# Attention weights of a graph network: one copy and one subtraction for a unit's transposed weights, where there were two of each

## The reference

```python
def _sparse_attention(x, src, dst, wq, bq, wk, bk, wv, bv, wo, bo):
    N, D = x.shape
    H, Dh = (NUM_HEADS, D // NUM_HEADS)          # 4 heads of 128
    q = (x @ wq + bq).reshape(N, H, Dh) * Dh ** (-0.5)
    k = (x @ wk + bk).reshape(N, H, Dh)
    v = (x @ wv + bv).reshape(N, H, Dh)
    scores = jnp.einsum('ehd,ehd->eh', q[src], k[dst])
    smax = jax.ops.segment_max(scores, src, num_segments=N)
    ex = jnp.exp(scores - smax[src])
    denom = jax.ops.segment_sum(ex, src, num_segments=N)
    attn = ex / denom[src]
    out = jax.ops.segment_sum(attn[:, :, None] * v[dst], src, num_segments=N)
    return out.reshape(N, D) @ wo + bo

for i in range(NUM_BLOCKS):                      # 4
    y = _cond_layer_norm(x, cond, s1_w[i], s1_b[i], b1_w[i], b1_b[i])
    x = x + _sparse_attention(y, src, dst, wq[i], ..., bo[i])
    y = _cond_layer_norm(x, cond, s2_w[i], s2_b[i], b2_w[i], b2_b[i])
    x = x + jax.nn.relu(y @ m_w1[i] + m_b1[i]) @ m_w2[i] + m_b2[i]
```

## Time and profile before

| | |
|---|---|
| median of 3 runs | 1796.01 us (1793.98 to 1800.16) |
| the profiled execution | 1803.08 us, of which the span from the first to the last instruction is 1801.3 us |
| mean granted TensorE clock | 0.988 of full speed |
| TensorE matmuls / weight loads busy | 1736.3 us (96%) / 1529.9 us (85%) |
| VectorE busy | 1244.6 us (69%) |
| ScalarE busy | 791.8 us (44%) |
| GpSimd busy | 588.7 us (33%) |
| subtraction of the weights, L1218 | 320 times, 243.9 us |
| copy of the weights, L982 | 320 times, 202.4 us |

### The profile page before, as it was taken

The page is one execution under the profiler, slowest core; times in us unless marked ns, Lnnn a source line. Parts: engine busy times, 40 slices in busy tenths (PEclk is TensorE's granted clock), DMA queues, the critical chain, the costliest instruction groups (busy, mean ns, idle before and its releaser), DMA issues.

```text
span 1801.3 us, 32290 instructions
## 1 busy us (share of the span) xinstructions
PE 1736.3 (96%) x11886; PEld 1529.9 (85%) x11886; DVE 1244.6 (69%) x2198; ACT 791.8 (44%) x1304; POOL 588.7 (33%) x892
## 2 busy tenths in 40 slices
PE   6999997899999999999999999999999999999998
PEld 5997786788999888879998888799987887999877
DVE  5998557736787668357776783577767835778676
ACT  4553432124666341246664412366644213666531
POOL 1003454402333534023334540123346401233383
PEclk9999998999999999999999999999999999999999
DMA  4002400221111212121212121211121122112221
GB/s 130 1 1 88 167 36 30 87 97 45 45 60 31 80 64 87 52 71 31 60 46 82 41 87 61 81 34 52 53 83 41 43 106 72 39 45 60 61 94 69
DMA packets 64714, 113.07 MB, mean 63 GB/s; under 512 B 15254, under 2 KB 25622, under 8 KB 64576
## 3 DMA queue, kind: packets, MB, share of 16 engines
q1 hardware_dynamic: 64576, 111.22, 19.1%
HBM read 89.19 MB, written 22.00 MB: 62 GB/s over the span
## 4 chain that ended last, share of the span: by engine, by line
PE 81%; DVE 10%; issue 4%; ACT 2%; DVEq 2%; POOL 1%; DMA 1%; SPq 0%; POOLq 0%; ACTq 0%
PE ps L1500 55%; PE ps L1561 14%; PE ps L1646 6%; PE ps L1587 2%; PE ps L1601 2%; DVE masked_s L1234 1%; DVE hot L1067 1%; DVE x L1271 1%; PE ps L1458 1%; DVE mask_log L1107 1%; DVE stat L1088 1%; DVE hot L1070 1%; DVE mask_out L1112 1%; ACT mask_log L857 1%; POOL rstd L637 1%
## 5 line engine op out<-in xcount | busy, mean ns | idle before, releaser
L1218 DVE TENSOR_TENSOR pT<-ps,pT 128x640 fp32r<-128x640 f32 (+1 forms) x320 | 243.9, 804 | 154.4 <-ACT pT L982 154.4
L1500 PE MATMUL ps<-yT,w 128*128 128x512 f32 (+1 forms) x1728 | 330.4, 352 | 1.3 <-DVE y L1355 1.3
L1500 PE MATMUL ps<-kh,q_parts 128*128 128x512 f32 (+3 forms) x1440 | 315.8, 363 | 10.2 <-DVE small L1234 7.0
L1500 PEld LDWEIGHTS ps<-yT,w 128*128 128x128 f32 x1728 | 280.5, 189 | 46.6 <-DVE y L1355 1.7
L982 ACT CAST pT<-ps 128x640 fp32r<-128x640 f32 (+1 forms) x320 | 202.4, 685 | 252.9 <-PE ps L1646 242.3
L1500 PEld LDWEIGHTS ps<-kh,q_parts 128*128 128x128 f32 (+1 forms) x1440 | 243.9, 185 | 58.2 <-issue 6.0
L1500 PE MATMUL ps<-w,kh 128*128 128x512 f32 (+1 forms) x960 | 240.5, 402 | 8.0 <-DVE x L1333 4.4
L1500 PEld LDWEIGHTS ps<-w,kh 128*128 128x128 f32 (+1 forms) x960 | 177.8, 190 | 48.4 <-DVE x L1333 5.3
L919 ACT ACTIVATE s<-masked_s,small 128x1280 f32 (+1 forms) x156 | 214.9, 1378 | 0.0
L1561 PE MATMUL ps<-pT,v 128*128 128x256 f32 (+1 forms) x1600 | 214.2, 280 | 0.0
L1561 PEld LDWEIGHTS ps<-pT,v 128*128 128x128 f32 x1600 | 199.5, 190 | 0.0
(11 more groups left out here) (188 smaller groups left out, 2596.2 us busy)
## 6 DMA issues: line engine op xcount, KB each, us to landing
mask<-mask_dram SPq DMA_DIRECT2D x24, 640.0 KB, 5.1
x_spill<-x SPq DMA_DIRECT2D x36, 256.0 KB
x<-x_spill SPq DMA_DIRECT2D x36, 256.0 KB, 4.6
rep<-rec_dram SPq DMA_DIRECT2D x64, 128.0 KB, 3.3
w_raw<-in_L_gnn_m_w_dram SPq DMA_DIRECT2D x8, 1024.0 KB, 6.0
mask_y<-mask_dram SPq DMA_DIRECT2D x12, 640.0 KB, 5.3
mask_dram<-mask_out SPq DMA_DIRECT2D x10, 640.0 KB, 2.9
x<-in_x_dram SPq DMA_DIRECT2D x2, 2304.0 KB
```

Source lines behind the costliest of these rows:

```text
L1218: nc.vector.tensor_tensor(pT[:, 1, places, k * P:k * P + R], turn_bank(half, R), pT[:, 0, places, k * P:k * P + R].bitcast(F32), ALU.subtr ...
L1500: mine = mm(to, left(a), right(b), start=first and n == 0, stop=final and n == 2)
```

## The change

The two halves are joined. ScalarE copies all 1280 columns of a unit in one instruction, and VectorE subtracts in one. Both use patterns that name the two runs of 640 columns in PSUM (`turn_banks`), and the two runs of five places in `pT` (`turned_weights`: a step of one half, or of two, by the parity of `gh`). Each semaphore now counts one for a unit instead of two, and TensorE's waits are rewritten: both parts of `weigh`, and both halves of the transposes, wait for the same count.

```diff
+        def turn_banks(R):
+            both = ps_flat[:, 3 * BANK:7 * BANK].rearrange("p (h b) -> p h b", h=2)[:, :, 0:NT // 2 * P]
+            return both.rearrange("p h (t r) -> p h t r", r=P)[:, :, :, 0:R]
+
+        def turned_weights(n, gh, k, R):
+            thirds = pT[:, n, :, :].rearrange("p (h t) r -> p h t r", t=NT // 2)
+            return thirds[:, 0:2 + gh % 2:1 + gh % 2, :, k * P:k * P + R]
...
                     act.wait_ge(turned, i * U + u + 1)
-                    for half in range(2):
-                        nc.scalar.copy(pT[:, 0, turned_places(gh, half), k * P:k * P + R], turn_bank(half, R)).then_inc(p_high, 1)
+                    nc.scalar.copy(turned_weights(0, gh, k, R), turn_banks(R)).then_inc(p_high, 1)
...
-                for half in range(2):
-                    places = turned_places(gh, half)
-                    dve.wait_ge(p_high, (i * U + u) * 2 + half + 1)
-                    nc.vector.tensor_tensor(pT[:, 1, places, k * P:k * P + R], turn_bank(half, R),
-                                            pT[:, 0, places, k * P:k * P + R].bitcast(F32), ALU.subtract).then_inc(p_ready, 1)
+                dve.wait_ge(p_high, i * U + u + 1)
+                nc.vector.tensor_tensor(turned_weights(1, gh, k, R), turn_banks(R), turned_weights(0, gh, k, R).bitcast(F32),
+                                        ALU.subtract).then_inc(p_ready, 1)
...
                 wd = rows(2 * g) + rows(2 * g + 1)
-                weights = (i * U + 2 * gh + 1) * 2 + part + 1
+                weights = i * U + 2 * gh + 2
                 pe.wait_ge(p_high, weights)
...
                         if u >= 1:
-                            pe.wait_ge(p_ready, (i * U + u - 1) * 2 + half + 1)
+                            pe.wait_ge(p_ready, i * U + u)
```

## The result

The changed kernel took 1808.97 us (median of 5 runs, 1807.74 to 1811.91), the kernel before 1794.40 us (5 runs, 1793.95 to 1800.16). The ratio is 1.0078, with a 95% interval of 1.0059 to 1.0097: slower by 0.6 to 1.0%, 14.6 us by the medians. (Against the 1796.01 us named ahead, the median of the first three of these runs, it is 13.0 us.) In a second comparison it was 1.0071 (1.0049 to 1.0094). The profiled execution of the changed kernel took 1807.74 us, its span 1806.0.

The account below looks back on a forecast made before the run. TensorE was taken as the bound, delayed by VectorE's later mask. Per block, 3.0 us for 16 pairs plus 0.9 for two dear pairs made 3.9, over four blocks 15.6: 1811.6 us on the median, range 1807 to 1816 (8-in-10: 1799 to 1822).

Parts of the forecast that it names:

- The bound, and who is late: In attention, TensorE bounds at 4.40 us a unit; its next scores wait for VectorE's mask, queued behind the subtraction.
- The lateness: The rest (copied value subtracted from the turned one) is ready 2.74 us after the copy's start, not 2.28: 0.46 later.
- The signal's time and the slack: Mask to TensorE's weight load: 0.12 us signal, leaving true slack of 0.37 after an even unit, 0.26 after an odd.
- Two short waits that do not add: Ordinary pair of units loses max(0.20, 0.09) = 0.20 us; the weighing's third-pass stall of 0.10 to 0.17 is absorbed.
- rival 2: Nothing absorbed: the weighing's 0.13 us stall adds to each pair's 0.20, giving 1820.8 us; chance 0.12.
- The dear pairs: Two pairs per block where VectorE also splits output-weight quarters ahead of the mask: no slack, the whole 0.46 us paid.
- The transposes' wait: TensorE's transposes waiting on the rest cost nothing: they load at 492.55, the rest is there at 491.99.
- The sum: Per block 16 x 0.19 = 3.0 plus 2 x 0.46 = 0.9, together 3.9 us; over four blocks 15.6 us.
- What I said the views would show: New trace: pair 9.0 us instead of 8.80, TensorE not busy throughout 82 us, mask and subtraction on the wait chain.
- rival 1: Slack covers ordinary pairs; only the dear pairs pay, 8 x 0.46 = 3.7 us, giving 1799.7 us; chance 0.15.
- rival 3: Joined two-piece operations save no fixed part: rest 0.77 us late, 9.7 us a block, 1834.8 us; chance 0.06.
- rival 4: Faster: the path from copy through exponential to transposes decides, each unit gains 0.06 us, 9.6 in all, 1786.4; chance 0.05.

Follow-up runs that it names:

- Both delays: Kernel before plus one unrelated VectorE maximum per unit ahead of the mask, over 128 or 384 columns: ratios 0.9991 and 1.0073.
- only the copy joined: Kernel before with ScalarE's copy joined into one instruction, VectorE still subtracting in two halves behind it: 1815.39 us, ratio 1.0098.
- The third trace: Unchanged kernel before, traced a third time to see whether half-clock stretches recur: 421.8 us ahead of the first attention stage.

## Why the prediction was right

The forecast was 15.6 us slower, 1811.6 us on the median; 1808.97 was measured, 14.6 us slower than the kernel before, and it lies in the forecast's own range of 1807 to 1816. By its steps:

**The bound, and who is late.** Right. The delay put into the kernel before shows it without the change: a mask 0.46 us later costs 16.2 of the 16.7 us in the stages, at unchanged copies, rests and waits.

**The two durations.** 1.23 and 1.485 us were taken, 1.230 and 1.492 measured.

**The lateness.** 0.46 us was forecast; 2.75 - 2.28 = 0.47 measured.

**The signal's time and the slack.** 0.12 us was taken for the signal, from a unit in mid-stage. The masks' signals against the weight loads give 0.10 behind every odd unit, so odd slack is 0.26 us. Both delays agree: 0.19 is free in ordinary pairs, and 0.46 costs 0.19 a pair on average.

**Two short waits that do not add.** 0.20 a pair was forecast, 0.20 measured (9.00 for 8.80). The stall at the third pass was there, 0.10 us, the low end of its 0.10 to 0.17, and it was inside the other wait: without it the pair is shorter by less than 0.01. So rival 2 falls. The wait was spread, in the changed kernel, almost evenly over both units (4.51 and 4.49), which I had not pictured; the sum is the same.

**The dear pairs.** 0.46 each was forecast, 0.49 measured.

**The transposes' wait.** It was put at nothing, from a unit in mid-stage. In the last unit of each block, where no scores come in between, that is wrong:

```profile
597.53 1.03 PE L1646 MATMUL ps<-ident,s 98*128 98x98 f32 x10 [0.99 <-ACT s L919]
```

```profile
596.46 1.01 PE L1651 MATMUL ps<-ident,s 98*128 98x98 f32 x10 [1.20 <-DVE pT L1223]
```

In the kernel before (first line) these transposes wait for the exponential, in the changed one for the rest of the unit before. The unit takes 3.94 us for 3.76, 0.7 us over the four blocks.

**The sum.** 3.9 us a stage was forecast, 4.2 measured. The two dear pairs have 0.98 of it for the forecast's 0.92, and everything else 3.2 for 3.0, the last unit's 0.18 included. The four stages have 16.7 us, and the time has 14.6; the missing 2 us lie outside attention, where executions differ by more than that. So the total came closer to the forecast than the stages alone make it: nothing was forecast outside attention, where the changed kernel met fewer half-clock stretches. For the forecast, that is luck.

**What I said the views would show** was wrong in two points: TensorE is still busy in all of the 82 us, and the mask is not on the chain of waits of ordinary units. The mechanism is there, and these views are too coarse for it.

The other rivals: the slack does not cover ordinary pairs (rival 1), the joined operations are not dearer (rival 3), and nothing ran through the exponential in mid-stage (rival 4). Rival 4's gain exists in the last unit of a block, where "only the copy joined" takes 3.71 us for 3.76.

## What to carry to other kernels

Two instructions that hand work from one engine to the next in halves overlap; joined, each engine works less and the result comes later. Before joining, follow the result to the engine that is the bound, through everything queued behind it on the way, and compare the added lateness with the slack there: here a lateness up to that slack was free, beyond it each pair of units paid the difference (0.47 - 0.26 forecasts 0.21, and 0.20 was measured), and two waits on one loop counted once. The cheap test is to delay the suspect by a foreign operation of known length, in two sizes, one below the slack and one above it.

## What the runs showed of the hardware that was not expected

The pattern of two pieces was a risk (rival 3) and cost nothing. A copy out of PSUM and a subtraction that read two runs of 640 columns, 1024 apart, and write ten pieces of 128, took 1.230 and 1.492 us: the copy as long as one that reads 1280 contiguous columns (1.229), and the subtraction within 2% of the mask operation of that size (1.470).

A TensorE wait of 0.1 us leaves no idle time in the busy shares nor in the chain of waits; it shows as a group of nine matmuls that is 0.09 us longer.

Stretches of 3.4 or 6.8 us at half the clock (1.2 GHz, where full clock is 2.4) came at the same few places of the program in some executions and not in others. In the first trace of the kernel before TensorE had stood idle for 2.18 us just ahead of the one at 141 us, and for 2.89 ahead of the one at 192. The third trace kept full clock at both. Most of the scatter between runs of one kernel goes with the mean granted clock: of the 62 timed executions of the kernel before that have one on record, those at 0.989 took 1803.4 to 1804.1 us, those at 0.992 took 1793.6 to 1797.9, those at 0.995 took 1793.5 to 1794.0.
